# Row maxima of the diagonal pieces masked on VectorE, batch norm inside the layer norm, ones written in strips

## What is computed

```python
def _L0_attn_b_ref(x, W_dq, W_uq, W_dkv, W_uk, W_uv, W_o):
    ...
    scores = jnp.einsum('bqhd,bkhd->bhqk', Q, K) / math.sqrt(D_K)
    causal = jnp.tril(jnp.ones((Sx, Sx), dtype=bool))
    scores = jnp.where(causal, scores, -jnp.inf)
    attn = jax.nn.softmax(scores, axis=-1)
    ...
def _L0_ffn_ref(inputs, gamma, beta, w_q, keys, key_in, key_out):
    ...
    mu = jnp.mean(x, axis=0)
    var = jnp.mean(jnp.square(x - mu), axis=0)
    xn = (x - mu) * jax.lax.rsqrt(var + BN_EPS) * gamma + beta
    q = (xn @ w_q.T).reshape(b, n, 2, h, kd).transpose(2, 0, 1, 3, 4)
    ...
```

## Time and profile before

| | us |
|---|---|
| median of 3 runs | 3712.21 (3711.64 to 3713.04) |
| the profiled execution, its own time | 3711.52 |
| its span in the profile | 3709.7 |
| first expert stage: layer norm's last statistics to the first scores | 419.04 to 435.43 |
| row maxima, first to last | 1609.0 to 2511.8 |

### The profile page before, as it was taken

The page is one execution under the profiler, slowest core; times in us unless marked ns, Lnnn a source line. Parts: engine busy times, 40 slices in busy tenths (PEclk is TensorE's granted clock), DMA queues, the critical chain, the costliest instruction groups (busy, mean ns, idle before and its releaser), DMA issues. The chain is left out here.

```text
span 3709.7 us, 76341 instructions
## 1 busy us (share of the span) xinstructions
PE 3226.0 (87%) x29442; PEld 2265.3 (61%) x29442; DVE 2972.4 (80%) x8985; ACT 1573.1 (42%) x2139; POOL 672.5 (18%) x308
## 2 busy tenths in 40 slices
PE   3997479999999985669999999998379999999997
PEld 2886357778787874423333333333257877878786
DVE  5443699999999995478888888881579999999996
ACT  1221244444444431424665666665144444444441
POOL 0000023333333331020000000000013333333333
PEclk6999699999999997879999999999699999999999
DMA  5535500000000002774222122002800000000000
GB/s 177 190 99 148 191 9 10 19 10 19 11 18 18 10 13 78 233 138 70 39 44 40 35 52 51 7 7 75 261 16 10 10 19 10 19 11 18 19 7 15
DMA packets 210446, 206.73 MB, mean 56 GB/s; under 512 B 50422, under 2 KB 186934, under 8 KB 208694
## 3 DMA queue, kind: packets, MB, share of 16 engines
q1 hardware_dynamic: 208182, 200.47, 19.5%
q10 hardware_dynamic: 1920, 1.57, 0.3%
HBM read 129.18 MB, written 72.42 MB: 54 GB/s over the span
## 5 line engine op out<-in xcount | busy, mean ns | idle before, releaser
L509 PE MATMUL f_p_route<-f_x_w,f_y_hot 128*128 128x64 f16 x8192 | 900.5, 194 | 85.1 <-DVE f_weighted L781 73.7
L533 PE MATMUL f_p_out<-f_kout,f_hidden 128*128 128x256 f16 x6144 | 857.2, 274 | 16.6 <-POOL f_hidden L436 15.9
L522 PE MATMUL f_p_hid<-f_xtc,f_kin_t 128*128 128x256 f16 x6144 | 855.3, 273 | 5.8 <-ACT f_hidden L621 5.7
L436 POOL TENSOR_TENSOR f_hidden<-f_weighted,f_hidden 128x1024 f16<-128x1024 f32 x256 | 610.2, 2384 | 1277.4 <-DVE f_x_w L771 1272.9
L1925 DVE TENSOR_REDUCE at_part_max<-at_p_ring 128x1 f32<-128x512 f32 (+3 forms) x1280 | 706.0, 603 | 119.9 <-PE at_p_ring L1794 75.5
L509 PEld LDWEIGHTS f_p_route<-f_x_w,f_y_hot 128*128 128x128 f16 x8192 | 692.7, 98 | 134.2 <-issue 108.5
L533 PEld LDWEIGHTS f_p_out<-f_kout,f_hidden 128*128 128x128 f16 x6144 | 603.1, 98 | 197.1 <-issue 118.6
L1905 ACT ACTIVATE at_prob<-at_p_s 128x1024 f32<-128x1024 f32 (+3 forms) x640 | 546.3, 895 | 388.3 <-PE at_p_s L1846 196.1
L522 PEld LDWEIGHTS f_p_hid<-f_xtc,f_kin_t 128*128 128x128 f16 x6144 | 602.3, 98 | 79.9 <-issue 10.3
L626 ACT CAST f_hidden<-f_weighted 128x1024 f16<-128x1024 f32 x256 | 343.4, 1341 | 587.5 <-DVE f_weighted L781 587.5
L621 ACT ACTIVATE f_hidden<-f_p_hid 128x512 f32<-128x512 f32 x512 | 301.0, 594 | 434.2 <-PE f_p_hid L522 433.5
(11 more groups left out here) (251 smaller groups left out, 3207.1 us busy)
## 6 DMA issues: line engine op xcount, KB each, us to landing
at_q<-qk SPq DMA_DIRECT2D x42, 256.0 KB, 4.5
at_k<-qk SPq DMA_DIRECT2D x42, 256.0 KB, 4.4
f_ln_xin<-x SPq DMA_DIRECT2D x16, 512.0 KB, 6.4
xt<-f_ln_xt SPq DMA_DIRECT2D x32, 256.0 KB, 5.2
f_kin_t<-kin_t SPq DMA_DIRECT2D x8, 1024.0 KB, 8.2
f_kout<-kout_parts SPq DMA_DIRECT2D x8, 1024.0 KB, 7.2
f_xt_in<-xt SPq DMA_DIRECT2D x32, 256.0 KB, 2.8
f_xres<-x SPq DMA_DIRECT2D x32, 256.0 KB, 2.7
```

The source lines that it names most:

```text
L436: nc.gpsimd.tensor_tensor(lo, weighted[s % WR], hi, ALU.subtract).then_inc(lo_ready, 1)
L509: last = nc.tensor.matmul(p_route[:, t, :], y_hot[:, s % HR, t // PAIR, :, t % PAIR], x_w[:, s % HR, half, t // PAIR, :, t % PAIR], start= ...
L522: last = nc.tensor.matmul(p_hid[g % 2][:, xp % 2, :], kin_t[:, a, dh, xp * P:(xp + 1) * P], xt[slot][:, b, dh, :], start=i % 6 == 0, stop= ...
L533: last = nc.tensor.matmul(p_out[:, u, :], parts[slot][:, xp, u * P:(u + 1) * P, a], kout[:, b, xp, :], start=g == 0 and i == 0, stop=xp == ...
```

## The change

1. The mask matmul is gone. A diagonal piece's maximum is now taken by `tensor_tensor_reduce`, which adds a mask from SBUF to the piece, writes the sum back to its PSUM bank and keeps the maximum. `mask_rows` grows to 512 columns of fp32, of which the last 128 hold the triangle, so that one slice fits each width.
2. Batch norm has no block of its own: its operations are appended to those of the layer norm on each engine, `gamma` and `beta` are loaded in the first turn, the identity and the first `xt_in` in the second. Their two semaphores and the four of batch norm are made before the layer norm instead of behind it.
3. The ones in `k` are written in 16 strips a slot, without the wait between slots.

What goes away beside it (`PAIRED`, `joint`, `column`, two semaphores) was not in use.

```diff
                 stores(NBLK - LNB + u, u)
+                if last_loads is not None and u == 0:
+
+                    sp.wait_ge(xt_stored[0], ONE + 16 * NK)
+                    last_loads(sp)
                 if prefetch is not None:
...
+            if last_root is not None:
+                last_root(act)
...
+            if last_statistics is not None:
+
+                dve.wait_ge(counted, ONE + NBLK)
+                last_statistics(dve)
...
-
+        ident, xt_in = sb("ident2", [P, P]), sb("xt_in", [P, DH, CH])
+
+        consts_loaded, xt_loaded = sem(tag + "consts_loaded"), sem(tag + "xt2_loaded")
...
-            layer_norm_pass(nc, sem, tag + "ln_", x_dram, xt_dram, ident_dram, bn_st, prefetch=load_weights)
...
+            def load_first_chunk(sp):
+                sp.dma_start(xt_in[:], xt_dram[0, :, :, :]).then_inc(xt_loaded, 16)
+                sp.dma_start(ident[:], ident_dram).then_inc(consts_loaded, 16)
+
+            def feature_root(act):
+            def feature_scales(dve):
...
+            def load_ahead(sp, turn, u):
+                load_weights(sp, turn, u)
+                if (turn, u) == (0, 0):
+                    with nc.allow_non_contiguous_dma(reason="512 scalars"):
+                        sp.dma_start(gb[:, 0, :], gamma.rearrange("(h p) -> p h", p=P)).then_inc(gb_loaded, 16)
+                        sp.dma_start(gb[:, 1, :], beta.rearrange("(h p) -> p h", p=P)).then_inc(gb_loaded, 16)
+
+            layer_norm_pass(nc, sem, tag + "ln_", x_dram, xt_dram, ident_dram, bn_st, prefetch=load_ahead,
+                            last_loads=load_first_chunk, last_root=feature_root, last_statistics=feature_scales)
...
-            sp.dma_start(ident[:], ident_dram).then_inc(consts_loaded, 16)
-            load_xt(0)
             load_xt(1)
...
-        mask_rows, mask_cols = sb("mask_rows", [P, P], BF16), sb("mask_cols", [P, P], BF16)
+        mask_rows, mask_cols = sb("mask_rows", [P, BLK]), sb("mask_cols", [P, P], BF16)
...
-            nc.gpsimd.affine_select(out=mask_rows[:], in_=mask_rows[:], compare_op=ALU.is_ge, fill=NEG, base=0,
+            nc.gpsimd.affine_select(out=mask_rows[:, BLK - P:BLK], in_=mask_rows[:, BLK - P:BLK], compare_op=ALU.is_ge, fill=NEG, base=0,
                                     pattern=[[-1, P]], channel_multiplier=1).then_inc(s["made"], 1)
...
             for i in range(SLOTS):
 
-                if i:
-                    pool.wait_ge(s["ones_set"], ONE + i)
-                else:
+                if i == 0:
                     pool.wait_ge(s["made"], ONE + 3)
-                nc.gpsimd.memset(k[i][KS_ROWS:KS_ROWS + M_ROWS, :, :], 1.0).then_inc(s["ones_set"], 1)
+                for h in range(HG):
+                    for c in range(QB):
+                        last = nc.gpsimd.memset(k[i][KS_ROWS:KS_ROWS + M_ROWS, h, c * BLK:(c + 1) * BLK], 1.0)
+                last.then_inc(s["ones_set"], 1)
...
-                diagonal = kb == qt // STEP
                 last = nc.tensor.matmul(bank[:, 0:cols], q[slot][0:KS_ROWS, h, qt * P:(qt + 1) * P],
-                                        k[slot][0:KS_ROWS, h, kb * BLK:kb * BLK + cols], start=True, stop=not diagonal)
-                if diagonal:
-                    last = nc.tensor.matmul(bank[:, cols - P:cols], identb[:], mask_rows[:], start=False, stop=True)
+                                        k[slot][0:KS_ROWS, h, kb * BLK:kb * BLK + cols], start=True, stop=True)
                 last.then_inc(s["turn_ready"], 1)
                 number += 1
...
                 one, cols = p_ring[number % RING], piece_columns(qt, kb)
-                if kind == "max":
-                    dve.wait_ge(s["turn_ready"], ONE + number + 1)
-                    nc.vector.reduce_max(part_max[qb][:, row, c:c + 1], one[:, 0:cols], axis=AX.X).then_inc(s["turn_taken"], 1)
-                    number += 1
+                dve.wait_ge(s["turn_ready"], ONE + number + 1)
+                if kb < qb:
+                    nc.vector.reduce_max(part_max[qb][:, row, kb:kb + 1], one[:, 0:cols], axis=AX.X).then_inc(s["turn_taken"], 1)
+                else:
+
+                    last = nc.vector.tensor_tensor_reduce(one[:, 0:cols], one[:, 0:cols], mask_rows[:, BLK - cols:BLK], 1.0, NEG,
+                                                          ALU.add, ALU.max, part_max[qb][:, row, kb:kb + 1])
+                    last.then_inc(s["turn_taken"], 1)
+                number += 1
...
+            dve.wait_ge(s["made"], ONE + 2)
             dve.wait_ge(s["ident_loaded"], ONE + 16)
             nc.vector.tensor_copy(identb[:], ident[:]).then_inc(s["made"], 1)
```

More of the change, by code:

```diff
@@ L293, in product_key_memory @@
             bn_var, bn_tmp, gb = fb("bn_var", [P, DH]), fb("bn_tmp", [P, DH]), fb("gb", [P, 2, DH])
-            layer_norm_pass(nc, sem, tag + "ln_", x_dram, xt_dram, ident_dram, bn_st, prefetch=load_weights)
             gb_loaded, bn_steps = sem(tag + "gb_loaded"), sem(tag + "bn_steps")
             bn_var_ready, bn_root_ready = sem(tag + "bn_var_ready"), sem(tag + "bn_root_ready")
-            block = first.enter_context(nc.Block())
-            @block.sync
-            def _(sp):
-                with nc.allow_non_contiguous_dma(reason="512 scalars"):
-                    sp.dma_start(gb[:, 0, :], gamma.rearrange("(h p) -> p h", p=P)).then_inc(gb_loaded, 16)
-                    sp.dma_start(gb[:, 1, :], beta.rearrange("(h p) -> p h", p=P)).then_inc(gb_loaded, 16)
-            @block.scalar
-            def _(act):
+            def load_first_chunk(sp):
+                sp.dma_start(xt_in[:], xt_dram[0, :, :, :]).then_inc(xt_loaded, 16)
+                sp.dma_start(ident[:], ident_dram).then_inc(consts_loaded, 16)
+            def feature_root(act):
                 act.wait_ge(bn_var_ready, ONE + 1)
                 nc.scalar.activation(scale[:], bn_var[:], ACT.Sqrt).then_inc(bn_root_ready, 1)
-            @block.vector
-            def _(dve):
+            def feature_scales(dve):
                 chain = Chain(dve, bn_steps)
@@ L324, in _, with routed_experts @@
                 chain.link(nc.vector.tensor_tensor(shift[:], gb[:, 1, :], bn_tmp[:], ALU.subtract))
[L326 to L331 removed]
+            def load_ahead(sp, turn, u):
[6 more added lines that the diff above has]
+                            last_loads=load_first_chunk, last_root=feature_root, last_statistics=feature_scales)
+        routed_experts(nc, sem, tag, x_dram, y_dram, xt_dram, ident, xt_in, wct, kin_t, kout, scale, shift,
+                       consts_loaded, xt_loaded, weights_loaded, kout_loaded, hidden)
+def routed_experts(nc, sem, tag, x_dram, y_dram, xt_dram, ident, xt_in, wct, kin_t, kout, scale, shift, consts_loaded,
+                   xt_loaded, weights_loaded, kout_loaded, hidden):
     with ExitStack() as ctx:
@@ L1444 @@
 LEAD, CATCH_UP = 0.58, 1.6
-PAIRED, JOINT = False, 2 * P
 def piece_columns(qt, kb):
@@ L1595, in attention_plan @@
     unit_weight = float(sum(weight)) / NU
-    def row_pieces(n, h, qt):
-        qb = qt // STEP
-        kbs, out = list(range(qb + 1)), []
-        while kbs:
-            kb = kbs.pop(0)
-            joint = PAIRED and bool(kbs) and piece_columns(qt, kb + 1) >= JOINT
-            if joint:
-                kbs.pop(0)
-            out.append(("joint" if joint else "max", n, h, qt, kb))
-        return out
     def block_pieces(n, qb):
-        return [p for h in range(HG) for qt in range(STEP * qb, STEP * qb + STEP) for p in row_pieces(n, h, qt)]
+        return [("max", n, h, qt, kb) for h in range(HG) for qt in range(STEP * qb, STEP * qb + STEP) for kb in range(qb + 1)]
     def cost(piece):
         kind, n, h, qt, kb = piece
-        return piece_columns(qt, kb) + 120 + (piece_columns(qt, kb + 1) + 120 if kind == "joint" else 0)
+        return piece_columns(qt, kb) + 120
     blocks = [(n, qb) for n in range(NU) for qb in range(QB)]
@@ L1627, in attention_plan @@
     first, one = last_of[AHEAD - 1] + 1, last_of[0] + 1
-    prologue = (pieces[:one] + [("r", 0)] if not PAIRED else pieces[:one + 3] + [("r", 0)] + pieces[one + 3:one + 3])
-    taken = one if not PAIRED else one + 3
-    prologue = prologue + pieces[taken:taken + 3] + [("m", 0)] + pieces[taken + 3:first]
+    prologue = pieces[:one] + [("r", 0)] + pieces[one:one + 3] + [("m", 0)] + pieces[one + 3:first]
     k, done, passed = first, sum(map(cost, pieces[:first])) / unit_cost, 0.0
@@ L1698, in unit_loaded @@
             eng.wait_ge(loaded[n % SLOTS], ONE + (n // SLOTS + (n % SLOTS != 0)) * 16 * N_LOADS)
-        def column(piece):
-            kind, n, h, qt, kb = piece
-            return (kb + 1) // 2 if PAIRED and qt // STEP >= 2 else kb
         @block.gpsimd
@@ L1823, in take_turns @@
                         turn_maxima(turn[1])
-                    elif turn[0] in ("max", "joint"):
+                    elif turn[0] == "max":
                         kind, n, h, qt, kb = turn
@@ L1830, in take_turns @@
                         row_scores(n, h, qt, kb)
```

(4 more changed lines are left out.)

14 lines of the change are left out of this document (4 added, 10 removed).

## The result

The changed kernel takes 3687.35 us, median of 4 runs (3683.31 to 3688.40); the kernel before took 3712.53 beside it (3711.64 to 3713.04). The ratio is 0.993, with a 95% interval of 0.9913 to 0.9948: 25 us less (19 to 32 by the interval), where 23.0 were forecast. Run again on another chip it gave 3683.64 us and a ratio of 0.9929 (0.9915 to 0.9942).

What follows compares the result with a forecast made beforehand. In the row maxima (902 us) VectorE was taken as ahead in 38% of pieces, TensorE in 62%. Terms -7.0 - 8.3 - 4.7 - 2.9 - 0.1 = -23.0 gave 3689 us as a median, range 3664 to 3708.

Steps and rivals of the forecast that it cites:

- Batch norm: Layer norm to experts' first scores: merging batch norm into the layer norm gives -7.0 in the first stage, -8.3 in the second.
- the 28th semaphore: Experts' block: ScalarE waits for base_ready, last but one of SP's 28 semaphores; xn starts 1.9 + 0.1 us after the opening.
- the opening of the experts' block: End of layer norm, first stage: the block opens once the stores land, at 424.8, 4.0 us earlier than at 428.87.
- Ones in strips: Attention's start: the first split's cast, held by GpSimd's long memset, is held by one strip at most: -4.7 us.
- The mask: Attention's row maxima: matmul removal and second instruction, -17.9 and +12.8 in the steps, +2.2 in the prologue, together -2.9.
- the second instruction: Diagonal pieces on VectorE: writing the maximum out costs 0.07 us each; +12.8 in the steps at a share of 0.38.
- the removal of the matmul: Main steps on TensorE: 480 mask matmuls of 0.06 us go, 0.62 of them on the path: -17.9 us.
- the prologue: Attention ahead of the main steps: VectorE is ahead on the path, so 32 second instructions of 0.07 cost +2.2 us.
- TensorE has the path: Rival, row maxima: the read is hidden or free, mask gives -26.6 in place of -2.9, 3665.5 us; chance 0.13.
- The read waits: Rival, row maxima: the read waits for the sum's end, 0.15 a piece, mask +14.3, 3706 us; chance 0.17.
- half rate: Rival, diagonal pieces: the in-place sum in PSUM streams at half rate, 0.40 us more a piece, 3755 us; chance 0.15.
- The merge gives only the block: Rival, expert stages: each gains only the block's 4.0 us, 2 x (-4.0 + 0.4) in place of -15.3, 3697 us; chance 0.10.

Runs made afterwards that it cites:

- mask_alone: The kernel before with only the mask moved to VectorE; batch norm's own block and the long memsets stay: 3706.4 us, ratio 0.9982.
- the three kernels above whose edits touch the expert stages only: Changed kernel with base_ready made ahead of the layer norm (3683.5 us), kout's four loads moved into the experts' block (3680.4 us), or both (3680.2 us).
- maxima_unmasked: Changed kernel with plain maxima on diagonal pieces, no mask matmul or sum, and queries scaled by a further 1/256: 3683.4 us, ratio 0.9922.

## Why the prediction came out right

**Batch norm, forecast -15.3.** Right in mechanism and nearly in size. In fourteen stages with the merge alone (seven traces) the mean is 61.7 us, in eight without it (four traces) 68.9: -7.2, and six more semaphores +0.35 (from the last store of the stage ahead to the first load 5.01 us before, 5.36 after; I said 0.4). Two stages give -13.7, and the kernel with the merge alone -14.5. All the steps stand in the trace: the chain hidden, no wait for `beta`, `xn` held by the 28th semaphore for 1.93 us (I said 1.9 + 0.1). The step that came out too large is the opening of the experts' block, for which I had taken over the landing of the last stores from the profiled execution of before; it accounts for the missing 1.6 us. Without the merge the next block opens 4.6 to 5.9 us behind the issue of the first of them (mean 5.1 of the eight stages), with it 6.0 to 7.1 (mean 6.4); my two stages had 5.9 and 5.0, 1.9 less in all than twice 6.4. That `kout` holds the stores is shown by its removal (4.56 in both stages); why they land later with the merge than without is not. The loads of `xt_in` and identity, put ahead of `kout` in the queue and priced at nothing (0.8 if their cover were gone), are the likely cause: behind them the first load of `kout` is issued 2.4 us after the fifth block's stores (408.44 against 406.05) where it was 1.25 before (404.95 against 403.70). No run took them alone.

**Ones in strips, forecast -4.7.** Shown: -4.6 by the run with this edit alone (interval of its ratio: 1 to 8), and -4.8 in its prologue.

**The mask, forecast -2.9.** Right in sign, too small by half; it gave 5.8 alone (interval of its ratio: 3 to 10). Both of its terms were mis-sized. The first is the second instruction. I priced it at 0.07 us a piece, from the load ahead of FIND_INDEX8. It holds the next piece for 0.01 to 0.02, and a sum that itself starts before another in-place sum has ended holds the next piece for 0.05 in all. The Trainium skill (VectorE: DVE Perf Modes) has a better rule than the one that I weighed: its section "Two Vector instructions with no wait between them" counts an accumulator read as an instruction that is held only where start quadrants change. Here they don't, and the trace agrees: 0.61. The 0.04 more behind another sum are not in that rule. The second term is the removal of the matmul, priced at a share of 0.62 of its 0.06 us.

The steps give the two prices apart (us; the mean where there are several traces):

| | plain maximum | sum on diagonal pieces | sum everywhere |
|---|---|---|---|
| no mask matmul | 914.65 | 915.3 (913.4 to 916.7, six traces) | 928 |
| one | 923.3 (921.1 to 925.1, three) | 928.5 | |
| two | 941.3 | | |

Taking the matmul away gave 8.65 us beside plain maxima and 13.2 beside sums, where I had 17.9. Adding one gave 18.0. The kernels with several traces scatter by 3 to 4 us, and 914.65, 928.5 and 941.3 are one trace each. The six traces are those of the changed kernel (twice), of `mask_alone`, and of the three kernels above whose edits touch the expert stages only. So it is clear that taking one away gave less than adding one cost, and not that it is worth more beside sums.

The sum cost 0.7 us without the matmul, within the scatter of the traces, and 5.2 with it; I had 12.8. Both of my terms were too large, by 4.7 to 9.3 and by 7.6 to 12.1 us, and in the sum they cancelled in good part. That is luck: with the second instruction at 0.01 and the share left at 0.62, I would have forecast -16 for the steps, twice what they gave. The total came within 2 us also because the merge fell short by about 1 us while the mask gave 3 more.

The term that I had put at nothing is TensorE's clock. Windows over the steps of the kernel before and of `maxima_unmasked` (the third number from the end is the mean granted clock):

```profile
1637.73:2561.42 923.69, 888.90 (x6225) 346.24 (x6223) 735.18 (x1485) 559.70 (x672) 0.00 (x0) 0.98 0.21 38
1625.56:2540.21 914.65, 875.52 (x5744) 319.68 (x5742) 731.88 (x1486) 559.30 (x672) 0.00 (x0) 0.97 0.21 39
```

Added up from the clock's records, this many us of the steps ran at the lower of its two levels, 1.2 GHz:

| | plain maximum | sum on diagonal pieces | sum everywhere |
|---|---|---|---|
| no mask matmul | 62.5 | 47.6 (43.9 to 51.2) | 52.7 |
| one | 35.0 (28.8 to 40.5) | 43.8 | |
| two | 31.7 | | |

The three traces of 921.1, 923.7 and 925.1 us had 28.8, 35.6 and 40.5 us of it, which is 0.35 us of time for each. At that price the 27.5 us more without matmul and sum cost 10 us (an estimate): at the clock of the kernel before, the removal would have given some 18, as much as the second matmul cost, and the sum would have cost some 6 without the matmul and 2 with it. That the clock is lower is no chance of one execution: the four runs of `maxima_unmasked` have a mean of 0.938 to 0.940 over the whole kernel, the twelve of the kernel before beside it 0.940 to 0.942. But no run holds the clock still, so it is not shown that this is where the removed work went. The waits of the earlier trace rows don't show the share of 0.62 in either case, since 449 of the 481 are the weight load's.

In the prologue I had +2.2 and the trace shows none: 39.96 with the mask alone against 40.00. There the long memset decides, since the cast ends with it whenever it starts (it took 5.58 us in that run, 5.14 before). With strips it is 35.16 with the matmul, 34.5 to 35.0 with the sum, 35.1 with both and 33.6 with neither: the sum costs 1.1 us alone and the matmul 1.5, and both together no more than the matmul.

**The rivals.** "TensorE has the path" is out as I priced it: the kernel without matmul and without sum, 3683 us, is its best case and reaches nowhere near 3665. Its premise is not refuted by that: TensorE is without a matmul for only some 35 to 40 us of the steps. "The read waits" and "half rate" are out by 0.61 us between starts. "The merge gives only the block" is out by the stages, 7.2 us shorter where it had 4.0, with `xn` 1.93 us behind the opening in place of 5.3.

**What the trace added by itself.** The profiled pair has +2.05 us in the unchanged memory stage (the +2.4 of the table less the 0.35 of six semaphores) and -1.8 in the second stage's unchanged experts. Over all traces the first load of `x` of the first expert stage lies between 366.9 and 369.7; a stage's shortfall of 2 us, as the second one's here (63.15, and 61.44 when run again), is not to be explained from one trace.

## What to carry to other kernels

Price a new instruction by the distance from one start to the next, not by its length, and look at what stands ahead of it: the same pair cost 0.01 us behind a plain maximum and 0.05 behind another sum. Where two engines take turns through a small ring of banks, split a count of waits by the instruction that waited before making a share of the path from it: here 449 of 481 waits were of weight loads. And look at the granted clock of the stretch before laying a difference to an instruction: here a second matmul for each diagonal piece cost 18 us and removing the only one gave 9 to 13, while TensorE, with less to do, ran at its lower clock for longer. What a stage waits for at a block's end is worth reading in full, loads queued ahead of the last store and semaphores set in a row included: here they were another 3.5 us a stage behind the 7.2 that the change took.

## What the hardware showed that was not expected

- A sum with maximum is two instructions in the trace, and the next piece's instruction starts in the same instant as the second of them, before the first has ended (1605.64 against 1605.00 + 0.73).
- VectorE reading and writing one PSUM bank in place streams at full rate: 695 ns for 512 columns against 685 for a plain maximum. Written to SBUF it is 682. The short instruction takes 139 ns behind an in-place sum and 81 behind one written to SBUF. A sum that starts before another in-place sum has ended is 0.73 us long and the next piece starts 0.65 behind it; with the sums written to SBUF it is 0.68 to 0.69 and 0.61.
- A cast of 16 x 128 elements took 5.1 to 5.6 us beside GpSimd's long memset, ending 0.08 us behind it in all four traces that have it, and 0.23 to 0.55 beside strips 0.47 apart, in ten.
- With the mask matmuls replaced by sums TensorE was granted less clock: 0.972 to 0.976 over the steps in six traces, against 0.978 to 0.984 in the three with the matmuls and plain maxima. One trace with neither has 0.966, one with both 0.976.
- A store of 256 KB of the layer norm lands in 3.7 us (median) where the 1 MB loads of `kout` don't stand among the stores, and in 5.2 (kernel before) to 6.3 (changed kernel) where they do. The last two stores of a stage, which hold the block open, take 4.2 to 6.0 us in the changed kernel and 2.5 to 3.4 with those loads moved behind.
